# Two layers of attention and experts on one core: the score chunks of a turn in one run over six PSUM banks

## The reference, cut to what matters

```python
x = L0_attn_x                                  # (8, 512, 256)
xn = layernorm(x)
x = x + attention(xn) + expert_ffn(xn)         # layer 0
xn = layernorm(x)
x = x + memory_read(xn) + routed_ffn(xn)       # layer 1

# attention: 16 heads of 64, q and k rms-normalised
scores = q @ k.T * scale + bias                # bias: -distance * slope * softplus gate of the key
attn = softmax(where(causal, scores, -inf))
y = attn @ v;  out = y @ Wproj
# expert_ffn: each of 32 experts takes its 8 best tokens of each batch row, merged into one
h = gelu(concat(merged, 1) @ w1[e]);  o = concat(h, 1) @ w2[e];  scattered back by the same weights
```

## Time and profile before

| | us |
|---|---|
| median of 3 runs | 1443.78 (1443.22 to 1446.7) |
| the profiled execution | 1444.28 |
| its span, first to last instruction | 1442.5 |
| TensorE busy in it | 1380.5 |
| VectorE busy | 991.6 |
| ScalarE busy | 915.8 |
| GpSimd busy | 168.4 |

### The profile page before, as it was taken

One profiled execution on the slowest core, in us unless ns is written; L12 is line 12 of the kernel. 1 busy time (PEld: TensorE's weight loads), 2 busy tenths in 40 slices (PEclk: granted clock), 3 DMA queues, 4 the chain that ended last, 5 costly groups with the idle time before them and its releaser, 6 DMA issues.

```text
span 1442.5 us, 28165 instructions
## 1 busy us (share of the span) xinstructions
PE 1380.5 (96%) x9680; PEld 1087.5 (75%) x9680; DVE 991.6 (69%) x3164; ACT 915.8 (63%) x2292; POOL 168.4 (12%) x562
## 2 busy tenths in 40 slices
PE   4779999999999999999999999999999799999998
PEld 3567778777777777787777777777777578888997
DVE  6938885888588768858875788588578665555442
ACT  5738784878488757848784877578577624433332
POOL 4501110110101101100110111011101100000000
PEclk8879999999999999999999999999999899999999
DMA  6542332232222313222231233132222212111100
GB/s 230 197 146 81 102 97 82 83 113 85 83 81 96 102 63 102 97 76 88 93 104 57 92 113 101 63 100 69 67 94 72 57 57 58 41 41 41 41 16 30
DMA packets 88303, 122.90 MB, mean 85 GB/s; under 512 B 8561, under 2 KB 74466, under 8 KB 88162
## 3 DMA queue, kind: packets, MB, share of 16 engines
q1 hardware_dynamic: 87842, 121.11, 26.1%
q10 hardware_dynamic: 320, 0.00, 0.0%
HBM read 101.69 MB, written 19.40 MB: 84 GB/s over the span
## 4 chain that ended last, share of the span: by engine, by line
PE 87%; ACT 4%; DVE 1%; issue 1%; DMA 0%; SPq 0%; ACTq 0%; DVEq 0%
PE at L799 19%; PE at L808 11%; PE at L884 10%; PE at L859 8%; PE at L925 8%; PE at L1471 7%; PE at L1507 6%; PE at L813 3%; PE at L911 2%; PE at L894 2%; PE at L851 2%; PE at L839 2%; PE at L844 2%; ACT L1065 1%; ACT probT L1056 1%; PE at L1490 1%
## 5 line engine op out<-in xcount | busy, mean ns | idle before, releaser
L1047 ACT ACTIVATE prob<-prob,low 128x512 f32<-128x512 f32 (+3 forms) x512 | 280.6, 550 | 70.9 <-DVE low L1180 70.8
L1180 DVE CUSTOM_DVE_ANT_0 prob<-at,mask 128x512 f32<-128x512 f32 (+3 forms) x512 | 220.5, 487 | 78.9 <-PE at L813 78.9
L1056 ACT ACTIVATE probT<-at 128x512 f32<-128x512 f32 (+1 forms) x256 | 131.6, 541 | 123.2 <-PE at L859 123.1
L808 PE MATMUL at<-kT,qT 64*128 64x512 f32 (+3 forms) x1024 | 194.2, 461 | 8.8 <-DVE up_lo L1233 5.0
L799 PE MATMUL at<-w_hi,cT_lo 128*128 128x386 f32 x512 | 197.5, 386 | 5.1 <-DVE area_raw L1129 4.3
L799 PE MATMUL at<-w_lo,cT_hi 128*128 128x386 f32 x512 | 175.0, 342 | 0.0
L799 PE MATMUL at<-w_hi,cT_hi 128*128 128x386 f32 x512 | 175.0, 342 | 0.0
L859 PEld LDWEIGHTS at<-ident,prob 128*128 128x128 f32 x1280 | 142.4, 141 | 40.0 <-issue 36.7
L859 PE MATMUL at<-ident,prob 128*128 128x128 f32 x1280 | 164.4, 275 | 2.1 <-DVE prob L1193 1.9
L1193 DVE TENSOR_SCALAR prob<-prob,rec 128x512 f32<-128x512 f32 (+3 forms) x512 | 163.3, 383 | 4.5
L884 PE MATMUL at<-probT,v 128*64 128x512 f32 (+3 forms) x1024 | 152.2, 439 | 0.1
(11 more groups left out here) (219 smaller groups left out, 2571.5 us busy)
## 6 DMA issues: line engine op xcount, KB each, us to landing
area_w<-in_L_ffn_w SPq DMA_DIRECT2D x64, 1024.0 KB, 5.5
bias<-in_L_ffn_w SPq DMA_DIRECT2D x160, 32.0 KB, 3.7
x_in<-in_L_attn_x SPq DMA_DIRECT2D x8, 512.0 KB, 6.4
xr<-in_L_attn_x SPq DMA_DIRECT2D x8, 512.0 KB, 4.1
eo_d<-eo SPq DMA_DIRECT2D x32, 128.0 KB, 1.8
x_d<-xr SPq DMA_DIRECT2D x8, 512.0 KB, 2.9
area_raw<-x_d SPq DMA_DIRECT2D x8, 512.0 KB, 4.1
out<-area_raw SPq DMA_DIRECT2D x8, 512.0 KB, 3.0
```

Of the source, the lines that this page charges most:

```text
L808: eng.matmul(bS[i][:, at:at + (c + 1) * P], qT[rows, c * P:(c + 1) * P], kT[rows, 0:(c + 1) * P], start=True, stop=False)
L1047: eng.activation(sl, sl, ACT.Exp, scale=-1.0, bias=low[:, i:i + 1], accum_out=den[:, i:i + 1]).then_inc(exp_done.sem, 1)
L1056: eng.activation(probT[h][:, x:y], bR[i][:, 0:y - x], ACT.Copy).then_inc(done.sem, 1)
L1180: eng.tensor_tensor_reduce(out=prob[s % 2][h][:, off[c]:off[c + 1]], in0=bS[i][:, at:at + (c + 1) * P], in1=mask[:, (NT - 1 - c) * P:T], s ...
```

## The change

The banks are dealt out anew. The eight score tiles of a turn get six banks (`bC`: the three of `bS`, then bank 2 of `bR`, 0 and 1), so all of them are computed in one run at the turn's start (`all_scores`). Head 0's transposes go to the banks `bS`, head 1's to `bR` (`bP`); each of their pieces waits for the `lows` that read its bank instead of for the other head's copies. y is now in a bank of `bS` (`bY`), and `turn_aug` waits no longer for y's copy. `hid` is turned into a bank of its own (`bH`). On TensorE project 1 stands behind project 0, and project 2 behind head 1's transposes, ahead of `values`. On VectorE all `lows` stand at the start with `mean_square` between them, the copies of the experts' hidden tile and output, and the bias addition, stand where the loop below shows. On ScalarE exps and gelu go ahead of head 0's copies, and the gate goes behind three chunks of exps.

```diff
-        bY = bR[2]
-        bX = bS[2]
-        bS = bS + [bQ[0]]
+        bY, bX, bH = bS
+        bP = (bS, [bR[2], bR[0], bR[1]])
+        bC = bS + [bR[2], bR[0], bR[1]]
...
-                 (2, 0): (1, 0), (2, 1): (0, 0), (0, 0): (1, 3 * P), (0, 1): (0, 3 * P)}
+                 (2, 0): (4, 0), (2, 1): (5, 0), (0, 0): (4, 3 * P), (0, 1): (5, 3 * P)}
...
-            area_y=area_y, area_w1=area_w1, area_w2=area_w2, bF=bS[0:2], bR=bS[2], bU=bQ, bD=bR[0:2], bMem=bR[2],
+            area_y=area_y, area_w1=area_w1, area_w2=area_w2, bF=bS[1:3], bR=bS[0], bU=bQ, bD=bR[0:2], bMem=bR[2],
...
-                def scores_3(s):
+                def all_scores(s):
                     eng.wait_ge(maxed.sem, maxed.at(s - 1))
-                    scores(3)
-
-                def scores_210(s):
+                    eng.wait_ge(y_done.sem, y_done.at(s - 2))
                     if begins_in(s - 1) is not None:
                         eng.wait_ge(biased.sem, biased.at(begins_in(s - 1)))
                     if s > 1 and ends_in(s - 1) is not None:
                         eng.wait_ge(eo_done.sem, eo_done.at(ends_in(s - 1)))
-                    eng.wait_ge(raw_D.sem, raw_D.at(s + 2 if s + 2 < NTURN else NTURN - 1))
-                    for n in jobs_at.get((s, 1), ()):
-                        eng.wait_ge(prep_done.sem, prep_done.at(n))
-                    scores(1)
-                    eng.wait_ge(maxed.sem, maxed.at(s, 2))
-                    if ends_in(s) is not None:
-                        eng.wait_ge(hidT_done.sem, hidT_done.at(ends_in(s)))
-                    scores(2)
-                    scores(0)
+                        eng.wait_ge(hidT_done.sem, hidT_done.at(ends_in(s - 1)))
+                    for c in (3, 1, 2, 0):
+                        scores(c)
...
-                    eng.wait_ge(y_done.sem, y_done.at(j - 2))
...
                 def turn_p0(s):
                     eng.wait_ge(p_done.sem, p_done.at(s, 1))
                     for i in range(3):
+                        if s + 1 < NTURN:
+                            eng.wait_ge(maxed.sem, maxed.at(s + 1, i + 1))
                         turn_p(s, 0, i)
 
                 def turn_p1(s):
                     eng.wait_ge(p_done.sem, p_done.at(s, 2))
-                    eng.wait_ge(pt0_A.sem, pt0_A.at(s, 1))
-                    turn_p(s, 1, 0)
-                    eng.wait_ge(pt0_D.sem, pt0_D.at(s))
-                    turn_p(s, 1, 1)
-                    eng.wait_ge(pt0_A.sem, pt0_A.at(s, 2))
-                    turn_p(s, 1, 2)
+                    for i in range(3):
+                        if s + 1 < NTURN:
+                            eng.wait_ge(maxed.sem, maxed.at(s + 1, (4, 7, 8)[i]))
+                        turn_p(s, 1, i)
 
                 def values(s):
                     eng.wait_ge(v_done.sem, v_done.at(s))
+                    eng.wait_ge(pt0_A.sem, pt0_A.at(s))
+                    eng.wait_ge(pt0_D.sem, pt0_D.at(s))
...
                 def hidden(m, s):
-                    eng.wait_ge(maxed.sem, maxed.at(s, 4))
+                    eng.wait_ge(maxed.sem, maxed.at(s, 2))
+                    eng.wait_ge(pt0_D.sem, pt0_D.at(s - 1))
...
                 def turn_hidden(m, s):
-                    eng.wait_ge(maxed.sem, maxed.at(s, 1))
+                    eng.wait_ge(pt0_A.sem, pt0_A.at(s - 1))
...
-                        scores_3(s)
+                        all_scores(s)
                     else:
                         eng.wait_ge(y_done.sem, y_done.at(s - 2))
+                        eng.wait_ge(eo_done.sem, eo_done.at(E - 1))
                     if s > 0:
                         turn_p0(s - 1)
                     if s + 2 < NTURN:
                         eng.wait_ge(o_done.sem, o_done.at((s - 1) // HP - 1))
                         project(s + 2, 0)
                     prepare(s, 0)
+                    if s + 2 < NTURN:
+                        project(s + 2, 1)
+                    prepare(s, 1)
                     if s > 0:
                         turn_p1(s - 1)
                     if ends_in(s) is not None:
                         turn_hidden(ends_in(s), s)
                     if s + 2 < NTURN:
-                        project(s + 2, 1)
-                    prepare(s, 1)
-                    if s < NTURN:
-                        scores_210(s)
+                        project(s + 2, 2)
+                    prepare(s, 2)
                     if s > 0:
                         values(s - 1)
                     if begins_in(s) is not None:
                         hidden(begins_in(s), s)
                     if ends_in(s) is not None:
                         expert_output(ends_in(s), s)
-                    if s < NTURN:
-                        eng.wait_ge(maxed.sem, maxed.at(s, 4))
-                    if s + 2 < NTURN:
-                        project(s + 2, 2)
-                    prepare(s, 2)
                     if s + 1 < NTURN:
+                        if s == 0:
+                            eng.wait_ge(maxed.sem, maxed.at(0, 8))
...
                 for s in range(NTURN + 1):
                     if s + 1 < NTURN:
                         square(s + 1)
-                    if s > 0:
-                        copy_p(s - 1, 0, 0)
-                        copy_p(s - 1, 0, 2)
                     if s % 4 == 2:
                         gelu(s // 4)
                     elif s < NTURN:
                         exps(s, 3)
+                        exps(s, 1)
+                    if s > 0:
+                        copy_p(s - 1, 0, 0)
+                        copy_p(s - 1, 0, 2)
                     prepare(s, 0)
+                    if s + 1 < NTURN:
+                        rsqrt(s + 1)
+                    if s + 2 < NTURN:
+                        take_raw(s + 2, 1)
+                    prepare(s, 1)
                     if s > 0:
                         copy_p(s - 1, 1, 0)
                         copy_p(s - 1, 1, 2)
-                    if s + 1 < NTURN:
-                        rsqrt(s + 1)
                     if s % 4 == 2:
                         exps(s, 3)
-                    prepare(s, 1)
-                    if s + 2 < NTURN:
-                        take_raw(s + 2, 1)
+                        exps(s, 1)
+                    if s < NTURN:
+                        exps(s, 2)
                     if s + 1 < NTURN:
                         gate(s + 1)
+                    if s + 2 < NTURN:
+                        take_raw(s + 2, 2)
+                    prepare(s, 2)
                     if s < NTURN:
-                        exps(s, 1)
-                        exps(s, 2)
                         exps(s, 0)
                     if s > 0:
                         copy_y(s - 1)
-                    prepare(s, 2)
-                    if s + 2 < NTURN:
-                        take_raw(s + 2, 2)
...
                 for s in range(NTURN + 1):
                     if s < NTURN:
                         lows(s, 3)
+                        lows(s, 1)
+                    if s + 1 < NTURN:
+                        mean_square(s + 1)
+                    if s < NTURN:
+                        lows(s, 2)
+                        lows(s, 0)
+                    if s + 2 < NTURN:
+                        take_raw(s + 2)
+                    prepare(s, 0)
                     if s > 0:
                         copy_p(s - 1, 0)
-                    if s + 2 < NTURN:
-                        take_raw(s + 2)
+                    prepare(s, 1)
                     if s + 1 < NTURN:
-                        mean_square(s + 1)
-                    prepare(s, 0)
+                        newton_step(s + 1)
                     if s > 0:
                         copy_p(s - 1, 1)
                     if ends_in(s) is not None:
                         copy_hidden(ends_in(s))
                     if s + 1 < NTURN:
-                        newton_step(s + 1)
                         gate_input(s + 1)
                         norm(s + 1)
                         gate(s + 1)
-                    prepare(s, 1)
-                    if s < NTURN:
-                        lows(s, 1)
-                        lows(s, 2)
-                        lows(s, 0)
                     if s < NTURN:
                         divide(s, 0)
                     if begins_in(s) is not None:
                         add_bias(begins_in(s))
                     prepare(s, 2)
+                    if ends_in(s) is not None:
+                        copy_expert_output(ends_in(s))
                     if s + 1 < NTURN:
                         copy_q(s + 1)
                     if s < NTURN:
                         divide(s, 1)
-                    if ends_in(s) is not None:
-                        copy_expert_output(ends_in(s))
                     prepare(s, 3)
```

18 lines of the change are left out of this document (9 added, 9 removed).

## The result

| | before | after |
|---|---|---|
| median of 4 runs each, on one chip | 1445.24 (1443.22 to 1450.04) | 1429.45 (1425.69 to 1434.56) |
| ratio to before, 95% interval | | 0.9885 (0.9849 to 0.9921) |
| span of the profiled execution | 1442.5 | 1424.1 |

A forecast was written before the change was run, and what follows sets the result against it. TensorE was taken to bound the loop, ScalarE's chain one turn in four, engine round trips the last two turns. Savings 4.6 + 3.8 + 4.9 + 4.6 - 1.1 + 1.5 = 18.3 us gave 1426.0 from 1444.28, range 1416 to 1439.

The forecast's parts named there:

- Gaps between blocks: Ordinary turns on TensorE: fewer losses between blocks of matmuls save 0.10 us per turn (bounds 0 to 0.26), 4.6 in all.
- No new wait in ordinary turns: Ordinary turns: the new order opens no wait, cost 0; thinnest cover 0.2 to 0.6 us, ahead of `values`.
- rival 1: VectorE takes over in every turn; `values` waits 0.5 us or more in 61 turns, 1456 us; chance 0.09.
- Gelu turns: 15 gelu turns before turn 62: two waits go, a 0.8 us wait at turn_aug comes; 0.25 saved each, 3.8 together.
- augment 1.59, T+13.75: Gate chain in gelu turns: from VectorE's gate part, augment needs 1.59 us, ending 13.75 us after the turn's start.
- First turn: First turn: the 2.64 us wait of `hidden` goes, waits for `take_raw` and at turn_aug come; 1.5 saved, bounds 0 to 2.6.
- The ends: Turns 62, 63 and 64: 4.9 and 4.6 us saved, 1.1 lost; bounds for the three together 3 to 13 saved.
- turns 62 and 63 still hold waits of 2 us and more: Sign in the last turns' windows that would show the forecast for the ends (part 3) wrong.
- Rival 2: TensorE's block order is free and gelu turns keep their length; only the ends win, 9.9 us, 1434.4; chance 0.20.
- with the blocks free alone: Variant where only TensorE's block order brings nothing, the other gains staying: 1429 us.
- Rival 3: The gate chain is longer and gelu turns grow by 0.6 us: 13 us back, 1439; chance 0.08.
- Rival 4: The gate chain does not hold TensorE at all: 0.7 us more saved in 15 turns, 1415.5; chance 0.05.

The follow-up runs named there:

- e_split: Kernel after, with TensorE's project 0 between score chunks 3, 1 and score chunks 2, 0, head 0's transposes following: 1448.21 us, one run.
- e_pr2_back: Kernel after, with TensorE's project 2 behind the experts' matmuls again, so values follows head 1's transposes at once: 1502.02 us, one run.
- e_div_late: Kernel after, with VectorE's divide(s, 0) in gelu turns behind the copies of the expert's output and of q: 1419.62 us, one run.
- e_gate: Kernel after, with ScalarE's gate in gelu turns behind the two exps of 512 columns, ahead of the other four: 1411.66 us, ratio to before 0.9767.
- e_prep: Kernel after, with the second slot of preparing jobs behind head 1's transposes and copies in turns 62 to 64: 1422.6 us, one run.
- e_pool: Kernel after, with GpSimd's second-layer constants waiting for turn 62's last division and its last two memsets for spread's copy: 1426.0 us, one run.

## Why the prediction was right, and where it was not

| term, us by spans | predicted | measured |
|---|---|---|
| 46 ordinary turns | 4.6 | 12.4 (0.27 each) |
| 15 gelu turns | 3.8 | 1.2 |
| first turn | 1.5 | 2.0 |
| turn 62 | 4.9 | 3.4 |
| turn 63 | 4.6 | 1.7 |
| turn 64 to the end of the last `values` | -1.1 | -2.3 |
| elsewhere | 0 | 0.0 |
| sum | 18.3 | 18.4 |

The first two rows together are turns 1 to 61, from 114.26 to 1120.42 before and from 112.43 to 1104.95 after. The stretch of turn 64 is 6.17 before (1158.67 to 1164.84) and 8.43 after (1138.20 to 1146.63).

- **Gaps between blocks: mechanism right, size off by a factor of 2.7.** The mis-sized step is "only one block of scores is left, so one loss in front of scores goes (0.10)". There are four losses of 0.1 around such a block, two of them inside the scores themselves, 0.22 in this change and put at nothing in the sum; `e_split` shows each. The new transitions, taken at 0.045 each, cost 0.07 each. The rows that I needed stood in the trace of before: four score matmuls of 256 columns behind project take 0.35 (549.88 to 550.23), as good as the four of 384 columns inside the run, 0.37 (550.53 to 550.90). Of the stated bounds, 0 to 0.26, the upper end was reached, but by a loss that the bounds hadn't in them: that is luck.
- **No new wait in ordinary turns: right.** They are busy throughout, and rival 1 didn't come. `e_pr2_back` shows that the cover was needed: take project 2 out of it, and the wait that rival 1 describes stands in every turn, 55.2 us in all.
- **Gelu turns: one wait takes the other's place, right; its length, wrong.** The step that failed is "augment 1.59, T+13.75". From the gate to `augment`'s end it now takes 2.05 (532.68 to 534.73), 0.46 more; the gate being 0.2 earlier than placed, TensorE goes on at T+14.05 (534.78) and the turn ends at T+15.7. I carried a duration over without asking what the other engine does beside it. `e_div_late` gives the 0.46 back, `e_gate` the rest.
- **First turn: right.** The wait of `hidden` is gone, the granted clock is 1.00 and not 0.88, and project 2 waits 1.42 for `take_raw` and the transposes of `ag` 0.64, as placed (1.3 and 0.7).
- **The ends: the direction right, the gain of the three about a third (2.7 against 8.4).** For turn 62 I had a wait of 1.7 for VectorE (measured 1.75), but no slow clock: behind that wait head 1's ten transposes take 2.34 instead of 1.25. `e_prep` leaves waits of 0.75 and 0.52 in its place, and the clock is 1.00. In turn 63 "the work is 11.3" held (busy 11.43), but TensorE waits 4 us and not 1.2. The collision of division and GpSimd's constants is 1.9 of that (`e_pool`). In turn 64 the wait before the last `values` is 2.46, not 1.1: of it 1.8 comes from the place of the preparing transposes (`e_prep`, 0.68 left). Of the same 2.46, `e_pool` takes away 0.6 without moving the transposes, by keeping GpSimd's last memsets off VectorE's small instructions. The prediction's sign "turns 62 and 63 still hold waits of 2 us and more" has come true if the waits of a turn are summed (3.4 and 4.0); no single one is above 1.8.
- **Rivals.** Rival 2 was right that the gelu turns nearly keep their length, and wrong that blocks are free; its 1429 "with the blocks free alone" is a slip, since 1426.0 + 4.6 is 1430.6. Rival 3's longer chain came, by 0.46 less the 0.2 by which the gate was earlier than placed, which is not far enough to make the gelu turns longer than before. Rival 4 didn't come: the gap before `ag` is there. A right sum with errors of +7.8, -2.6, +0.5, -1.5, -2.9 and -1.2 in its terms is partly luck: the blocks gave back what the gelu turns and the ends missed. The range from 1416 to 1439 came from the terms' bounds and would have held most of their combinations.

## What to carry to other kernels

Where one engine is busy throughout, count its blocks of unlike matmuls: here a change between project and scores costs about 0.2 us, half at the end of the one block and half at the start of the next, and a block of scores too many costs 0.39 in every turn. When an instruction moves, look at what the other engine of the pair VectorE and GpSimd does beside its new place: here a duration read where the neighbour worked out of PSUM did not hold beside one from SBUF to SBUF. When a wait is removed from a chain, move the chain's next link forward in the same edit; here that was the gate, and it was worth 14.5 us in the gelu turns, where the whole change had won 13.6 in turns 1 to 61.

## What the runs showed of the hardware

- VectorE's divisions, from SBUF to SBUF, slow GpSimd's small instructions from 0.20 to 0.31, and GpSimd's memset and affine selects slow VectorE's divisions from 1.14 to 3.12 for four, each of the two small ones from 0.28 to 1.11 or 1.12. What VectorE read from PSUM beside the same small instructions, the `lows` of before and the copy of q in `e_div_late`, left them at 0.20 or 0.21.
- After a wait of 1.75 us in turn 62 the granted clock fell (0.90 over the turn), and after one of 1.87 before the last `values` of e_pool it fell too (0.57). After one of 2.46 at the same place in the kernel after, and after one of 1.87 at the start of turn 64 in the kernel before, it did not.
